# Two layers of attention and one of aggregation on one core: sums copied and finished later in the last layer, and another order at the seam between the attention layers

## The reference, cut to what matters

```python
def _gat_layer(h, adj, W, b):
    att = h @ h.T / sqrt(e)
    A = softmax(where(adj > 0, att, NEG), axis=1) * 0.5
    A = A.at[d, d].add(0.5)
    # rows below nf1 = sum(adj[:, 0] != 0): the identity's row
    return relu(A @ (h @ W.T + b))

h = maximum(layernorm(x), 0)
x = x + gat_layer(gat_layer(h, adj, W0, b0), adj, W1, b1)
h = maximum(layernorm(x), 0)
a_hat = adj + eye(4096)
a_norm = a_hat * d_inv_sqrt[:, None] * d_inv_sqrt[None, :]
out = x + (a_norm @ h) @ W.T + b
```

## Time and profile before

| | |
|---|---|
| time, median of 3 runs | 988.83 us (988.74 to 990.11) |
| the profiled execution | 988.96 us, span 987.1 us |
| TensorE matmul busy | 955.0 us (97%), 6598 matmuls |
| VectorE busy | 537.9 us (54%) |
| ScalarE busy | 443.8 us (45%) |
| GpSimd busy | 72.5 us (7%) |
| granted TensorE clock, mean | 0.994 |
| the seam | about 444 to 470 us of the span |
| the last layer | 842 to 987 us of the span |

### The profile page before, as it was taken

One profiled execution on the slowest core, in us unless ns is written; L12 is line 12 of the kernel. 1 busy time (PEld: TensorE's weight loads), 2 busy tenths in 40 slices (PEclk: granted clock), 3 DMA queues, 4 the chain that ended last, 5 costly groups with the idle time before them and its releaser, 6 DMA issues.

```text
span 987.1 us, 16183 instructions
## 1 busy us (share of the span) xinstructions
PE 955.0 (97%) x6598; PEld 869.3 (88%) x6598; DVE 537.9 (54%) x970; ACT 443.8 (45%) x641; POOL 72.5 (7%) x67
## 2 busy tenths in 40 slices
PE   3999999999999999998999999999999999999997
PEld 2999999999999999998999999999999999777776
DVE  3555444453535353535555675665666678844443
ACT  4655666666666666641111211211212222675664
POOL 3761000000000000003200000000000000000000
PEclk9899999999999999999999999999999999999999
DMA  9876998898898999860000000000000001300000
GB/s 257 209 165 173 201 227 211 212 222 221 207 234 199 231 206 229 204 205 2 1 2 3 12 12 1 11 12 11 12 1 12 22 12 33 118 1 33 20 13 24
DMA packets 105039, 103.24 MB, mean 105 GB/s; under 512 B 72960, under 2 KB 83968, under 8 KB 104960
## 3 DMA queue, kind: packets, MB, share of 16 engines
q1 hardware_dynamic: 104448, 101.94, 41.4%
q10 hardware_dynamic: 432, 0.20, 0.1%
q0 software_dynamic: 80, 0.02, 0.1%
HBM read 77.48 MB, written 7.86 MB: 86 GB/s over the span
## 4 chain that ended last, share of the span: by engine, by line
PE 94%; DVE 2%; DMA 2%; ACT 1%; SPq 0%; issue 0%; DVEq 0%; ACTq 0%
PE pAcc L1145 36%; PE pMisc L1212 10%; PE pS L1064 9%; PE pS L1062 9%; PE pS L1063 9%; PE pS L1236 6%; PE pS L1237 6%; PE pTurn L1199 5%; DMA adjT<-nat 1%; PE pMisc L1221 1%; DVE prob L938 0%; ACT aggT L614 0%; DMA chunk<-in_adj_dram 0%; ACT adj_wide L607 0%; PE pTurn L1157 0%
## 5 line engine op out<-in xcount | busy, mean ns | idle before, releaser
L1145 PEld LDWEIGHTS pAcc<-feat,prob 128*128 128x128 f32 x3200 | 382.6, 192 | 20.9 <-DVE prob L917 6.3
L1145 PE MATMUL pAcc<-feat,prob 128*128 128x129 f32 x3200 | 393.8, 276 | 7.1 <-DVE prob L917 5.8
L917 DVE TENSOR_TENSOR prob<-prob,adjT 128x1024 f32<-128x1024 f32 x128 | 156.8, 1225 | 201.8 <-ACT prob L555 195.9
L575 ACT ACTIVATE prob<-pS 128x1024 f32<-128x1024 f32 x72 | 73.8, 1024 | 309.0 <-PE pTurn L1199 273.3
L555 ACT ACTIVATE prob<-pS 128x1024 f32<-128x1024 f32 x128 | 130.9, 1022 | 141.2 <-PE pS L1064 141.0
L1062 PE MATMUL pS<-high 128*128 128x512 f32 x400 | 174.8, 437 | 0.0
L1064 PE MATMUL pS<-high,low 128*128 128x512 f32 x400 | 158.5, 396 | 0.0
L1063 PE MATMUL pS<-low,high 128*128 128x512 f32 x400 | 156.7, 392 | 0.0
L511 ACT ACTIVATE nat<-chunk 128x1024 uint8<-128x1024 f32 x128 | 134.4, 1050 | 12.5 <-DMA adjT<-nat 10.2
L1212 PE MATMUL pMisc<-feat,turned_prob 128*128 128x129 f32 x896 | 118.4, 275 | 0.0
L1212 PEld LDWEIGHTS pMisc<-feat,turned_prob 128*128 128x128 f32 x896 | 113.1, 191 | 4.7 <-DVE tiny_row L719 0.2
(11 more groups left out here) (119 smaller groups left out, 537.9 us busy)
## 6 DMA issues: line engine op xcount, KB each, us to landing
chunk<-in_adj_dram SPq DMA_DIRECT2D x128, 512.0 KB, 4.6
x_in<-in_x_dram SPq DMA_DIRECT2D x8, 256.0 KB, 6.1
adjT<-nat SPq DMA_TRANSPOSE x128, 3.6
x_block<-in_x_dram SPq DMA_DIRECT2D x8, 256.0 KB, 2.8
x_scratch<-mixed SPq DMA_DIRECT2D x8, 256.0 KB, 2.2
x<-x_scratch SPq DMA_DIRECT2D x8, 256.0 KB, 5.1
hiT_scratch<-highT SPq DMA_DIRECT2D x7, 256.0 KB, 5.0
loT_scratch<-lowT SPq DMA_DIRECT2D x7, 256.0 KB, 4.9
```

The lines of the kernel that those rows point to most:

```text
L917: nc.vector.tensor_tensor(pr, pr, adj_unit(b, u), ALU.mult).then_inc(prob_ready[L], 1)
L1145: mm = nc.tensor.matmul(pAcc[:, t // 2, (t % 2) * W:(t % 2 + 1) * W], prob[:, buf, h, t * P:(t + 1) * P], feat[:, 2 * u + h, :], start=(fi ...
```

## The change

In the last layer ScalarE copies a block's sum at `late` SLOTS − 1 = 5 instead of 1, and VectorE finishes a block at 9 instead of 7. TensorE's order there stays.

At the seam, `make_feat(1, 0)` stands ahead of the last mix of the first attention instead of behind it. Groups 1, 2 and 3 go to `pAcc` bank 0, `pAcc` bank 1 and `pTurn` instead of `pTurn`, `pAcc` bank 0 and `pAcc` bank 1. With that the wait for the copied `pAcc` goes from group 2 to group 1, group 3 gets a wait for the low part of the last block, and the turning of the last block loses its wait for `keep_feat(1, 1)`. On VectorE `keep_feat(1, 1)` stands behind `low_of_h1` instead of ahead of the largest norm.

```diff
         def feat_bank(L, grp):
-            return pMisc[:, :] if L == 0 else (pMisc[:, :], pTurn[:, :], pAcc[:, 0, :], pAcc[:, 1, :])[grp] if grp < 4 else (pMisc, pTurn)[grp % 2][:, :]
+            return pMisc[:, :] if L == 0 else (pMisc[:, :], pAcc[:, 0, :], pAcc[:, 1, :], pTurn[:, :])[grp] if grp < 4 else (pMisc, pTurn)[grp % 2][:, :]
...
-                    if after_block(k, 1) is not None:
-                        keep_agg(after_block(k, 1))
+                    if after_block(k, SLOTS - 1) is not None:
+                        keep_agg(after_block(k, SLOTS - 1))
...
             keep_feat(1, 0)
             norms(last, 1)
-            keep_feat(1, 1)
             dve.wait_ge(epi_step[0], NB * EPI[0])
             nc.vector.tensor_reduce(largest[:, :], norm[:, :], AX_X, ALU.max).then_inc(norm_top, 1)
             low_of_h1(last)
+            keep_feat(1, 1)
             dve.wait_ge(norm_turned, 1)
...
-                    if after_block(k, 7) is not None:
-                        finish(after_block(k, 7))
+                    if after_block(k, 9) is not None:
+                        finish(after_block(k, 9))
...
                 else:
-                    if grp == 2:
+                    if grp == 1:
                         pe.wait_ge(acc_kept[0], NB)
+                    if grp == 3:
+                        pe.wait_ge(h1_low, NB)
                     if grp >= 4:
...
                 wait(pe, h1_low, b)
-                if b == NB - 1:
-                    pe.wait_ge(feat_ready[1], 2)
                 for t in range(RT):
...
                             turn_h1(b - 1)
+                        if g == NB * UNITS - 1:
+                            make_feat(1, 0)
                         mix(L, b, u, u % 2, g)
...
             attention(0)
-            make_feat(1, 0)
             pe.wait_ge(exp_ready[0], NB * UNITS)
             first_scores(0)
             make_feat(1, 1)
```

## The result

| | before | changed |
|---|---|---|
| time, median of 5 runs | 988.83 us (987.52 to 990.11) | 978.84 us (978.48 to 980.19) |
| ratio, 95% interval | | 0.9888 (0.9864 to 0.9913) |
| the profiled execution | 988.96 us, span 987.1 | 980.19 us, span 978.4 |
| mean granted clock in it | 0.994 | 0.996 |

The change is faster. The medians are 10.0 us apart, and the ratio, taken against the executions of before on the same chip, makes it 11.1. The ratio's interval, 8.6 to 13.4 us, still holds 8.8, so this measurement alone doesn't show that a term is missing; the experiments do.

What follows compares the result with a forecast made beforehand. TensorE held 94% of the chain of waits, so only its pauses paid. Last layer 6.9 plus seam 1.9 gave 8.8 us off the profiled 988.96: 980.1 us as a median, within 979.3 to 981.0 (0.68); wider range 978.2 to 983.3.

Steps and rivals of the forecast that it cites:

- 8.8: Whole kernel: forecast gain in us, 6.9 from the last layer plus 1.9 from the seam.
- The last layer, 6.9 us: Seven block ends in the last layer: stall and slower restart of 0.99 us each regained, 6.9 us in all.
- The cover of the copy: Last layer: 1.1 us spare between the moved copy and the projection, so the move was costed at nothing.
- The finish's move: Last layer: VectorE's finish goes behind one more widening at each block end, costed at nothing.
- The seam by its waits, 1.92 us: Between the layers: turning released earlier, first mix of layer 2 at 460.2 instead of 462.10, gain 1.92 us.
- The early group 0: Seam: twelve matmuls ahead of the last mix start it 0.55 us late and end it 0.45 late.
- The sum, "6.9 + 1.9 = 8.8": Last layer plus seam, taken from the profiled 988.96 us: 980.2, or 980.1 us as a median.
- The clock: Rival: shifted pauses change the granted clock, 978.4 us if the one at 848 escapes, 981.8 if the seam's is caught; 0.12.
- The fall near 848: Clock drop after the 2.01 us pause ending at 848.29, costed at 1.7 us; escaping it would give 978.4 us.
- The base: Starting time: profiled execution 988.96 us, 0.13 above the median of 988.83, used to turn 980.2 into 980.1.
- The rule of the skill: Clock: activity is observed free-running, not tied to kernel start, so a 1.9 us shift may move either pause across the line.

Runs made afterwards that it cites:

- e4: Changed kernel with ScalarE's copy of a block's sum at 9 instead of 5: 983.29 us, ratio 0.993.
- e6: Changed kernel with VectorE's finish put back at 7: 978.57 us (four runs), ratio 0.9873.
- e3: Changed kernel with group 0 made behind the last mix again: median 978.41 us, ratio 0.9884, one execution of 5284 us left out.
- e5: Kernel before with ten unread matmuls filling TensorE's 2.4 us pause before the last block's turning: 988.85 us, ratio 0.9982.
- e9: Kernel before with two unread sums added on VectorE, to lengthen TensorE's pause before the last block's turning: 992.24 us.
- e2: Kernel before with only the seam part of the change, last layer as before: 986.51 us, ratio 0.9955.
- e1: Kernel before with only the last layer's places changed (copy at 5, finish at 9): 981.99 us, ratio 0.9908.
- e12 to e16: Kernel before, unchanged, run again for more traces: profiled executions took 989.16, 992.30, 995.87, 992.21 and 991.50 us.

## Why the prediction failed at the edge

- **The last layer, 6.9 us.** Right: 6.96 in the traces. The half alone has medians 989.68 − 981.99 = 7.7 apart, and the interval of its ratio, 5.8 to 12.4 us, holds 6.9. The cover of the copy was right too (`e4`). The finish's move I cost at nothing, and it is nothing (`e6`).
- **The seam by its waits, 1.92 us.** Right: 1.85, with each instant on the way within 0.1 us. The early group 0 costs 0.5 (`e3`), as worked out.
- **The sum, "6.9 + 1.9 = 8.8".** Right for what it summed: the lowest runs are 986.86 and 978.48, 8.4 apart. It left out a term of the kernel before.
- **The clock, the step that failed.** I wrote that the seam's stretch "shows 1.00", took the longer pause as uncaught, gave a fall at the seam only to the changed kernel, as a rival, and said that the shrinking pause speaks against it. The runs showed the reverse case to be the common one: the old pause was caught in six of seven traces, at 1.3 to 1.5 us and once 6.6, and it was the first trace that was the exception. So the sum put the old seam's clock at nothing, on one trace. The change takes this fall away together with the wait (`e5` and `e9` show that the pause brings it). The fall near 848 is gone from the traces too, a case that I had given 0.06, at 1.7 us (measured 1.5). The seam's half is worth 3.2 us by medians, not 1.9, and the 1.3 beyond the waits holds both falls, since `e2`'s trace has neither.
- **The base.** "0.13 above the median" leaned on three runs. The median of 70 more was 989.7, and 989.7 − 978.84 = 10.9 is the change's effect: 8.8 of waits, and by subtraction 2.1 for the clock, 1.3 of it in `e2` and 0.8 in `e1`, where it is within the noise.
- **The rule of the skill.** The Trainium skill (TensorE: Matmul & The Clock Gate, part on the HAM clock gate) calls the observation free-running, and the same pause being caught in one execution and not in the next agrees with that (`e12` to `e16` against the first trace). Whether the place in the execution matters as well stays open: of the changed kernel, `e2`, `e4` and `e6` no run of 29 is below 0.995, and with 2 us of shift three of six are at 0.994, but so are two of five of `e3`, without any shift to later.

## What to carry to other kernels

A copy that empties a finished accumulator belongs behind the ring fills that can be made before the accumulator is done (here two more, with a ring of six); its cover is the time to the first reader of the copy, and past that the delay is paid at every block (0.54 us with four more). A pause of TensorE costs more than its length when the granted clock falls behind it, and one trace can't show how often that happens: look at the mean clock of every run, and count a removed pause like these (2.0 and 2.4 us) as its waits plus the share of runs that fall times what a fall costs. A base of three runs is too narrow for a forecast to 0.5%.

## What the hardware showed that I had not expected

- The same pause of 2.38 to 2.39 us at the seam left the clock at 2.4 GHz in one trace and let it fall in six. A fall costs 1.3 to 1.5 us there, and cost 2.4 behind a pause of 3.7; in 15 of 70 runs of the kernel before the mean clock was 0.986 to 0.988, and the one such execution that was traced stood at the lower level for about 17 us, from 453.7 to 470.7, with TensorE busy behind the pause, and lost 6.6 us.
- Ten matmuls whose results nobody reads (2.45 us in the trace) removed that tail (0 of 12 runs at 0.992 or less, against 7 of 17) and delayed nothing.
- The same pause of 2.0 us near 848 was caught in seven of nine traces in which it ended at 848.29 us or later, and in none of seven in which it ended at 847.80 or earlier. The first nine have the old seam and the seven the changed one, so this isn't yet a rule of its place.
